# Two loops written out, and the halo copies shared between ScalarE and SyncE, in a four-layer convolution network

## The chip, the cores and the metric

The kernel runs on one core of one Trainium2 chip. Its engines are TensorE (PE in the profile; PEld is its weight load), VectorE (DVE), ScalarE (ACT), GpSimd (POOL) and SyncE (SP), which run side by side, each through its own list of instructions, and meet at semaphores. ScalarE and SyncE can also issue DMA transfers (ACTq, SPq). The metric is the device time of one execution in microseconds; lower is better.

## What is computed

The input is 64 images of 16 channels of 128 x 128 in float32. Four layers follow, each `x = x + f(group_norm(x))`, with eight groups of two channels:

```python
x = x + _L0_conv_ref(_gn(x), 5)      # Newton-Schulz inverse of each 128 x 128 matrix, 5 steps
x = x + _L1_conv_ref(_gn(x), ...)    # 3 x 3 convolution of x quantised with one scale for the whole batch
x = x + _L2_conv_ref(_gn(x), ...)    # convolution with five taps on a diagonal, zero padding
x = x + _L3_conv_ref(_gn(x), ...)    # circular 3 x 3 convolution (the reference takes it through FFTs)
```

Layer 1's scale is a maximum over all images, so layer 0 must be done for all of them before layer 1 starts for the first.

## The kernel before, in words

There are two blocks, one after the other.

The first does layer 0 image by image: `X` has four buffers (`SLOTS`), an image is 16 matrices of 128 x 128. TensorE multiplies (`products`, line 758; `last_products`, line 768), ScalarE takes the products out of PSUM (line 363), GpSimd forms the factor 2I - Y (line 288), the DVE finishes the image (line 528) and prepares the norms of the next (lines 425 to 482), whose broadcast on TensorE is line 742. SyncE loads image i+3 (line 243) and stores image i to a scratch tensor in device memory (line 249). Every engine runs the same function `step` for images 0, then a loop over images 1 to 60, then images 61 to 63. The loop (`images`, lines 80 to 85) is a hardware loop: `Fori` runs its body with a register, and the body has `turn` steps, here four, so it has 15 turns. Inside it, semaphore counts and addresses that depend on the image are computed in registers.

The second does layers 1 to 3 as a pipeline: at step s, image s is in layer 1, image s-1 in layer 2 and image s-2 in layer 3. The function `run` (lines 879 to 885) does steps 0 to 3, loops over steps 4 to 61 in turns of two, and does steps 62 to 65. An image lies in SBUF with 128 partitions = 8 rows x 16 channels, and 16 such blocks of rows in the free dimension. A convolution is a sum of matmuls in PSUM: the taps inside a block (line 1147), and then one product with the halo, the rows just above and below each block (line 1154). The halo lies in `xh`, six groups of 16 partitions, filled by six SBUF-to-SBUF copies: three groups from the block above, three from the block below. All six are issued by ScalarE in `halos` (line 939), for layer 3 after the circular wrap of the edges (`wrap`), for layer 1 when the DVE has quantised the next image (line 1003), for layer 2 when GpSimd has written the lower half of the fp16 split (line 920). ScalarE's other work in a step is a root for each norm (line 962), the upper half of the split (line 957), and a bias (line 969). SyncE only loads image s+2 from the scratch tensor (line 897) and stores image s-2 (line 908).

The order on each engine is the order written in its `step`. On TensorE it is: layer 1, layer 2, layer 3, each in four banks, with the small matmuls of the norm statistics (lines 1160 and 1165) put in between.

Of the kernel before, what the change touches and what calls it, by code (L numbers as in the profile page):

```python
# [20 lines left out]
C = 16  # L21
G = 8
CPG = C // G
RB = 8
NJ = H // RB
PW = H + 4
L = 2
# [7 lines left out]
SLOTS = 4  # L35
# [10 lines left out]
def conv_net(nc, x, ident, gmat, gsel, w1, w1h, w2, w2h, w3, w3h, scale_w, bias, x1d, out):  # L46
# [6 lines left out]
    B = x.shape[0]  # L53
# [23 lines left out]
        def wait(self):  # L77
            self.eng.wait_ge(self.sem, self.at)

    def images(eng, step, first, last, turn):  # L80

        assert (last - first) % turn == 0
        with eng.Fori(0, (last - first) // turn) as t:
            for a in range(first, first + turn):
                step(t * turn + a, t + a // turn, a % turn)

    keep = ExitStack()
    with keep:
# [36 lines left out]
        xn = [None] + [[persistent(f"xn{l}_{n}", [H, parts[l], FLAT], kinds[l]) for n in range(2)] for l in (1, 2, 3)]  # L125
# [15 lines left out]
        with mem:  # L141
# [80 lines left out]
            A_FIRST, A_LAST = 1, 3  # L222

            def image_steps(eng, step):

                for i in range(A_FIRST):
                    step(i, 0, i)
                images(eng, step, A_FIRST, B - A_LAST, SLOTS)
                for i in range(B - A_LAST, B):
                    step(i, i // SLOTS, i % SLOTS)  # L230

# [4 lines left out]
            with nc.Block() as block:  # L236

                @block.sync
                def _(sp):
                    def load(n, h, slot):  # L240
                        stand(sp, x1_stored[slot], 16 * h, const_loaded, 16 * 5)
                        stand(sp, reached, n - 3, const_loaded, 16 * 5)
                        sp.dma_start(X[slot][:, :, :], x[n, :, :, :]).then_inc(x_loaded[slot], 16)

                    def step(i, h, slot, last=False):
                        if not last:
                            load(i + 3, h + (slot + 3) // SLOTS, (slot + 3) % SLOTS)
                        stand(sp, out_ps, QUADS * (i + 1), const_loaded, 16 * 5)
                        sp.dma_start(x1d[i, :, :, 0:H].rearrange("j (r c) w -> (j r) c w", c=C),
                                     X[slot][:, :, :]).then_inc(x1_stored[slot], 16)  # L250

                    for t, s in ((idt, ident), (gm, gmat), (gs, gsel), (swt, scale_w), (bst, bias)):
                        sp.dma_start(t[:, :], s).then_inc(const_loaded, 16)
                    load(0, 0, 0)
                    load(1, 0, 1)
                    load(2, 0, 2)
                    for l, body, rows in ((1, w1, w1h), (2, w2, w2h), (3, w3, w3h)):
                        sp.dma_start(wf[l][:, :, :], body).then_inc(w_loaded, 16)
                        sp.dma_start(whf[l][:, :], rows).then_inc(w_loaded, 16)
                    for i in range(A_FIRST):  # L260
                        step(i, i // SLOTS, i % SLOTS)
                    images(sp, step, A_FIRST, B - A_LAST, SLOTS)
                    for i in range(B - A_LAST, B):
                        step(i, i // SLOTS, i % SLOTS, last=i + 3 >= B)
                    for n in range(SLOTS):
                        sp.wait_ge(x1_stored[n], 16 * (B // SLOTS))
# [568 lines left out]
        RUN = NJ * PW - (PW - H)  # L835
        HALO1 = [(-1, d, 0) for d in (-1, 0, 1)] + [(RB, d, RB - 1) for d in (-1, 0, 1)]
        HALO = (None, HALO1, HALO2, HALO1)
        with ExitStack() as mem:
# [7 lines left out]
            xh = [None] + [[sb(f"xh{l}_{n}", [6 * C, parts[l], NJ * PW], kinds[l]) for n in range(2)] for l in (1, 2, 3)]  # L846
# [16 lines left out]
            normed = [None] + [sem(f"normed{l}") for l in (1, 2, 3)]  # L863
            wrapped = sem("wrapped")
# [12 lines left out]
            FIRST = 4  # L877

            def run(eng, step):

                for s in range(FIRST):
                    step(s, s // 2, s % 2)
                images(eng, step, FIRST, B - 2, 2)
                for s in range(B - 2, B + 2):
                    step(s, s // 2, s % 2)

            def there(i):

                return not isinstance(i, int) or 0 <= i < B

            with nc.Block() as block:

                @block.sync
                def _(sp):
                    def load(n, h, odd):
                        stand(sp, evac[1], BPI * (n - 1), w_loaded, 16 * 6)
                        sp.dma_start(xs[1][odd][:, :, :],
                                     x1d[n, :, :, 0:H].rearrange("j p w -> p j w")).then_inc(x1_in[odd], 16)

                    load(0, 0, 0)  # L900
                    load(1, 0, 1)

                    def step(s, h, odd):
                        if there(s + 2):
                            load(s + 2, h + 1, odd)
                        if there(s - 2):
                            stand(sp, evac[3], BPI * (s - 1), w_loaded, 16 * 6)
                            sp.dma_start(out[s - 2, :, :, :], xs[3][odd][:, :, :]).then_inc(out_stored[odd], 16)

                    run(sp, step)  # L910
                    for n in range(2):
                        sp.wait_ge(out_stored[n], 16 * (B // 2))
# [19 lines left out]
                @block.scalar  # L932
                def _(act):
                    def halos(l, n, odd):

                        for k, (row, shift, _) in enumerate(HALO[l]):
                            r, at = (row + RB, 0) if row < 0 else (row - RB, 2 * PW)
                            at += L + shift
                            act.dma_start(xh[l][odd][C * k:C * k + C, :, 0:RUN],  # L939
                                          xn[l][odd][C * r:C * r + C, :, at:at + RUN]).then_inc(halo[l][odd], 16)  # L940

                    def wrap(i, odd):

                        v = xn[3][odd][:, :, :].rearrange("p s (j w) -> p s j w", w=PW)
                        link = Link(act, wrap_chain, 2 * i)
                        act.wait_ge(normed[3], i + 1)
                        link.done(nc.scalar.activation(v[:, :, 1:NJ + 1, L - 1], v[:, :, 1:NJ + 1, L + H - 1],
                                                       ACT.Copy))
                        link.done(nc.scalar.activation(v[:, :, 1:NJ + 1, L + H], v[:, :, 1:NJ + 1, L], ACT.Copy))
                        link.wait()  # L950
                        nc.scalar.activation(v[:, :, 0, :], v[:, :, NJ, :], ACT.Copy).then_inc(wrapped, 1)
                        nc.scalar.activation(v[:, :, NJ + 1, :], v[:, :, 1, :], ACT.Copy).then_inc(wrapped, 1)

                    def upper(l, n, odd):

                        act.wait_ge(scaled_f[l], n + 1)
                        nc.scalar.activation(padded(xn[l][odd], 0)[:, 1:NJ + 1, L:L + H], F[l][:, :, :],  # L957
                                             ACT.Copy).then_inc(high[l], 1)

                    def root(l, n):  # L960
                        act.wait_ge(gvar_sb[l], n + 1)
                        nc.scalar.activation(cols[l]["sd"][:, :], cols[l]["ve"][:, :],  # L962
                                             ACT.Sqrt).then_inc(groot[l], 1)

                    def first(n, h, odd):

                        act.wait_ge(normed[1], n + 1)
                        halos(1, n, odd)
                        nc.scalar.activation(xs[1][odd][:, :, :], xs[1][odd][:, :, :], ACT.Identity,
                                             bias=bst[:, 0:1]).then_inc(biased, 1)  # L970

                    def step(s, h, odd):
                        if there(s - 2):
                            wrap(s - 2, odd)
                            act.wait_ge(wrapped, 2 * s - 2)
                            halos(3, s - 2, odd)
                        if there(s):
                            root(2, s)
                            upper(2, s, odd)
                        if there(s + 1):  # L980
                            first(s + 1, h + odd, 1 - odd)
                        if there(s):
                            act.wait_ge(normed[2], s + 1)
                            halos(2, s, odd)
                        if there(s - 1):
                            root(3, s - 1)
                            upper(3, s - 1, 1 - odd)

                    first(0, 0, 0)
                    run(act, step)  # L990
# [263 lines left out]
```

## Time and profile before

| | us |
|---|---|
| three runs, median (lowest, highest) | 4625.2 (4619.82, 4630.58) |
| the profiled execution | 4624.59 |
| its span, first to last instruction | 4622.8 |
| mean granted TensorE clock | 0.986 of full |

The page of the profile begins with the busy time of each engine, then the span in 40 equal slices (busy share in tenths; PEclk is the granted clock of TensorE):

```profile
PE 4399.1 (95%) x24265; PEld 3045.4 (66%) x24265; DVE 3833.0 (83%) x8224; ACT 2251.8 (49%) x4551; POOL 2610.2 (56%) x2957
...
PE   7999999999999999999999599999999999999998
...
PEclk9999999999999999999999799999999999999999
DMA  1111111111111111211111365555556555555554
```

The first block fills some 22 slices, the second the rest. Of the queues of the page, q1 and q10 are data transfers, q8 and q14 instructions being fetched:

```profile
q1 hardware_dynamic: 284112, 269.46, 18.2%
q10 hardware_dynamic: 49152, 129.59, 16.8%
q8 instruction: 165, 2.70, 0.2%
q14 instruction: 162, 1.33, 0.1%
```

The chain of work that ended last, by engine:

```profile
PE 39%; DVE 3%; issue 1%; ACTq 0%; DMA 0%; ACT 0%; POOLq 0%; POOL 0%
```

### The profile page before, as it was taken

The page shows a single profiled execution, that of the slowest core. Times are in us where ns is not written, and L with a number is a line of the kernel's source. Part 1 is how long each engine was busy: PE and PEld are TensorE (multiplying, and loading weights), DVE is VectorE, ACT ScalarE, POOL GpSimd, SP SyncE. Part 2 cuts the span into 40 slices and gives each one's busy share as a digit, 9 for nine tenths or more (in the row PEclk, how much of TensorE's full clock was granted, in tenths as well). Part 3 has the DMA queues.
Part 4 walks back from the last instruction along what each step waited for, and adds up shares of the span by engine and source line. Part 5 has one row for each costly group of instructions (what it writes and reads, how often), then busy time and mean ns, then how long its engine had stood idle before and what let it go on. Part 6 is the DMA issues. An engine that isn't in the chain of part 4 may idle for free. (4 is left out here: it accounts for less than half of the span.)

```text
span 4622.8 us, 79863 instructions
## 1 busy us (share of the span) xinstructions
PE 4399.1 (95%) x24265; PEld 3045.4 (66%) x24265; DVE 3833.0 (83%) x8224; ACT 2251.8 (49%) x4551; POOL 2610.2 (56%) x2957
## 2 busy tenths in 40 slices
PE   7999999999999999999999599999999999999998
PEld 6888888888888888888888244444444444444443
DVE  7988898889888988988896687787787778778774
ACT  4766776777677766777776122222222222222221
POOL 7888888888888888888887122222222222222221
PEclk9999999999999999999999799999999999999999
DMA  1111111111111111211111365555556555555554
GB/s 59 61 48 56 56 56 56 56 56 56 56 56 56 56 56 47 63 49 56 56 56 37 84 137 130 130 134 137 125 132 139 127 130 136 132 128 134 137 127 85
DMA packets 333591, 403.08 MB, mean 87 GB/s; under 512 B 23088, under 2 KB 286032, under 8 KB 316880
## 3 DMA queue, kind: packets, MB, share of 16 engines
q1 hardware_dynamic: 284112, 269.46, 18.2%
q10 hardware_dynamic: 49152, 129.59, 16.8%
q8 instruction: 165, 2.70, 0.2%
q14 instruction: 162, 1.33, 0.1%
HBM read 135.22 MB, written 134.22 MB: 58 GB/s over the span
## 5 line engine op out<-in xcount | busy, mean ns | idle before, releaser
L288 POOL TENSOR_TENSOR M<-two,YX 128x256 f32<-128x256 f32 x2560 | 1827.0, 741 | 402.6 <-ACT YX L363 373.4
L758 PE MATMUL bank<-YX,M 128*128 128x256 f32 x8192 | 1948.5, 386 | 40.1 <-issue 40.1
L1147 PE MATMUL bank<-xn,wt 128*128 128x512 f16 (+1 forms) x6912 | 1660.2, 381 | 25.6 <-DVE xn L1003 17.9
L758 PEld LDWEIGHTS bank<-YX,M 128*128 128x128 f32 x8192 | 1504.1, 192 | 227.3 <-issue 44.5
L363 ACT ACTIVATE YX<-bank 128x512 f32<-128x512 f32 x2048 | 1227.5, 599 | 690.8 <-PE bank L758 684.8
L920 POOL TENSOR_TENSOR xn<-F,xn 128x2048 f16<-128x2048 f32 x128 | 487.8, 3811 | 1577.6 <-ACT xn L957 1577.6
L1147 PEld LDWEIGHTS bank<-xn,wt 128*128 128x128 f16 (+1 forms) x6912 | 672.9, 100 | 810.5 <-issue 18.8
L1021 DVE SCALAR_TENSOR_TENSOR x<-bank,wu,x 128x512 f32<-128x512 f32 x512 | 382.2, 746 | 294.7 <-PE bank L1154 283.8
L1154 PE MATMUL bank<-xh,wth 96*128 96x512 f16 (+1 forms) x1792 | 515.4, 380 | 15.3 <-DMA xh<-xn 15.3
L957 ACT ACTIVATE xn<-F 128x2048 f16<-128x2048 f32 x128 | 244.7, 1912 | 475.1 <-DVE F L1077 475.1
L410 DVE BATCH_NORM_STATS2 st<-X 128x6 f32<-128x256 f32 x1024 | 367.8, 410 | 9.6 <-DMA X<-in_x 9.6
L471 DVE TENSOR_SCALAR W<-X,m,r 128x256 f32<-128x256 f32 x512 | 363.3, 778 | 12.3 <-DVE r L463 12.1
L1032 DVE BATCH_NORM_STATS2 bs<-x 128x6 f32<-128x512 f32 x512 | 355.5, 694 | 17.6
L962 ACT ACTIVATE sd<-ve 128x1 f32<-128x1 f32 x128 | 26.0, 203 | 692.6 <-issue 363.0
L1154 PEld LDWEIGHTS bank<-xh,wth 96*128 96x128 f16 (+1 forms) x1792 | 174.4, 97 | 235.1 <-DMA xh<-xn 18.0
L354 ACT ACTIVATE YX<-bank,cs 128x128 f32<-128x128 f32 x1024 | 318.0, 389 | 10.7 <-DVE cout L497 10.0
L528 DVE SCALAR_TENSOR_TENSOR X<-bank,cout,X 128x128 f32<-128x128 f32 x1024 | 270.5, 342 | 40.6 <-PE bank L768 40.6
L282 POOL TENSOR_TENSOR W<-W 128x512 f16<-128x512 f32 x256 | 298.3, 1166 | 6.0 <-ACT W L332 6.0
L339 ACT ACTIVATE AD<-X,nm 128x256 f32<-128x256 f32 x512 | 256.7, 503 | 33.4 <-DVE nm L428 33.4
L768 PE MATMUL bank<-YX,M 128*128 128x128 f32 x2048 | 250.4, 280 | 0.0
L768 PEld LDWEIGHTS bank<-YX,M 128*128 128x128 f32 x2048 | 238.4, 192 | 3.3
L729 PE MATMUL bank<-W 128*128 128x128 f16 x3072 | 215.2, 220 | 2.3 <-ACT YX L354 2.3
(107 smaller groups left out, 3580.6 us busy)
## 6 DMA issues: line engine op xcount, KB each, us to landing
xh<-xn ACTq DMA_DIRECT2D x768, 131.8 KB, 4.3
X<-in_x SPq DMA_DIRECT2D x64, 1024.0 KB, 4.8
x_scratch<-X SPq DMA_DIRECT2D x64, 1024.0 KB, 5.7
x<-x_scratch SPq DMA_DIRECT2D x64, 1024.0 KB, 6.1
out<-x SPq DMA_DIRECT2D x64, 1024.0 KB, 3.8
xh<-xn ACTq DMA_DIRECT2D x384, 65.9 KB, 2.4
wf<-in_w SPq DMA_DIRECT2D x2, 192.0 KB, 8.5
wf<-in_w SPq DMA_DIRECT2D x1, 320.0 KB, 8.5
```

The lines of the kernel that those rows point to most:

```text
L288: nc.gpsimd.tensor_tensor(M[odd][:, at, :], two[:, :].unsqueeze(1).broadcast_to([H, 2, H]), YX[odd][:, at, 0:H], ALU.subtract).then_inc(ma ...
L354: ins = nc.scalar.activation(YX[odd][:, mat, 0:H], bank[:, m * H:(m + 1) * H], ACT.Copy, scale=cs[odd][:, mat:mat + 1])
L363: nc.scalar.activation(YX[odd][:, 2 * p:2 * p + 2, :], banks[u % A_RING][:, :].rearrange("p (m w) -> p m w", m=2), ACT.Copy).then_inc(yx_n ...
L410: ins = nc.vector.bn_stats((st0, st1)[k][:, g, :], group_of(X[slot], g))
L471: ins = nc.vector.tensor_scalar(group_of(W, g), group_of(X[slot], g), m0[:, g:g + 1], r0[:, g:g + 1], ALU.subtract, ALU.mult)
L758: ins = nc.tensor.matmul(banks[u % A_RING][:, 2 * H * m:2 * H * (m + 1)], M[odd][:, 2 * p + m, :], YX[odd][:, 2 * p + m, :], start=True, s ...
L768: ins = nc.tensor.matmul(banks[q][:, H * m:H * (m + 1)], M[odd][:, 4 * q + m, :], YX[odd][:, 4 * q + m, H:2 * H], start=True, stop=True)
L920: nc.gpsimd.tensor_tensor(padded(xn[l][odd], 1)[:, 1:NJ + 1, L:L + H], F[l][:, :, :], padded(xn[l][odd], 0)[:, 1:NJ + 1, L:L + H], ALU.sub ...
L1021: nc.vector.scalar_tensor_tensor(out=dst, in0=bank, scalar=wtop[l]["u"][:, 0:1], in1=xs[l][odd][:, a:b, :], op0=ALU.mult, op1=ALU.add).the ...
L1032: nc.vector.bn_stats(bst_[l][:, u, :], xs[l][odd][:, 4 * u:4 * u + 4, :]).then_inc(gchain[l], 1)
L1147: nc.tensor.matmul(bank, wt[l][:, a, k, :], v, start=(k == a == b == 0), stop=False)
L1154: ins = nc.tensor.matmul(bank, wth[l][:, a, :], v, start=False, stop=(a, b) == products[-1])
```

## The change

`images` is now a loop of the program that writes the kernel: each of the 60 images of the first block and the 58 steps of the second stands in the instruction lists by itself, with constant semaphore counts and addresses. No hardware loop is left in these two places. In the second block the copies of the block above stay with ScalarE, and the three copies of the block below are issued by SyncE, which waits for the same events. The sum of the copies on each halo semaphore is as before.

```diff
-    def images(eng, step, first, last, turn):
-
-        assert (last - first) % turn == 0
-        with eng.Fori(0, (last - first) // turn) as t:
-            for a in range(first, first + turn):
-                step(t * turn + a, t + a // turn, a % turn)
+    def images(step, first, last, turn):
+
+        for i in range(first, last):
+            step(i, i // turn, i % turn)
...
                 def _(sp):
+                    def halos(l, n, odd):
+
+                        if l == 3:
+                            sp.wait_ge(wrapped, 2 * n + 2)
+                        else:
+                            sp.wait_ge(normed[l], n + 1)
+                        for k, (row, shift, _) in enumerate(HALO[l][3:]):
+                            r, at = row - RB, 2 * PW + L + shift
+                            to = C * (k + 3)
+                            sp.dma_start(xh[l][odd][to:to + C, :, 0:RUN],
+                                         xn[l][odd][C * r:C * r + C, :, at:at + RUN]).then_inc(halo[l][odd], 16)
+
...
                     load(1, 0, 1)
+                    halos(1, 0, 0)
 
                     def step(s, h, odd):
+                        if there(s - 2):
+                            halos(3, s - 2, odd)
                         if there(s + 2):
                             load(s + 2, h + 1, odd)
+                        if there(s + 1):
+                            halos(1, s + 1, 1 - odd)
+                        if there(s):
+                            halos(2, s, odd)
                         if there(s - 2):
                             stand(sp, evac[3], BPI * (s - 1), w_loaded, 16 * 6)
                             sp.dma_start(out[s - 2, :, :, :], xs[3][odd][:, :, :]).then_inc(out_stored[odd], 16)
...
-                        for k, (row, shift, _) in enumerate(HALO[l]):
-                            r, at = (row + RB, 0) if row < 0 else (row - RB, 2 * PW)
-                            at += L + shift
+                        for k, (row, shift, _) in enumerate(HALO[l][:3]):
+                            r, at = row + RB, L + shift
                             act.dma_start(xh[l][odd][C * k:C * k + C, :, 0:RUN],
                                           xn[l][odd][C * r:C * r + C, :, at:at + RUN]).then_inc(halo[l][odd], 16)
```

## Rows read from the trace of the kernel before

**Rows 1.** Busy time by stretch: us, each engine's busy us (instructions), clock, DMA share, GB/s.
```profile
3000.00:3500.00 500.00, 488.04 (x2308) 224.01 (x2307) 396.87 (x784) 119.36 (x144) 121.95 (x32) 1.00 0.58 132
```

**Rows 2.** Timeline of SyncE (start, duration, operation): stores of images 0, 3, 4, 5, 60.
```profile
88.31 0.65 SPq L249 DMA_DIRECT2D x_scratch<-X  x1
...
203.01 0.57 SPq L249 DMA_DIRECT2D x_scratch<-X  x1
...
240.56 0.56 SPq L249 DMA_DIRECT2D x_scratch<-X  x1
...
282.79 0.56 SPq L249 DMA_DIRECT2D x_scratch<-X  x1
...
2428.03 0.57 SPq L249 DMA_DIRECT2D x_scratch<-X  x1
```

**Rows 3.** Waits of TensorE, 88 to 2426 us: total us, times, longest.
```profile
PE bank L758 <- issue: 40.1, 17, 3.1
PE bank L742 <- DVE ndiag L482: 26.2, 26, 1.0
```

**Rows 4.** Timeline of TensorE across a jump back: start, duration, in brackets idle before.
```profile
235.74 3.19 PE L768 MATMUL bank<-YX,M 128*128 128x128 f32 x26
...
241.70 3.63 PE L758 MATMUL bank<-YX,M 128*128 128x256 f32 x8 [2.77 <-issue]
```

**Rows 5.** Busy time in the stretch behind that jump; the clock is third from last.
```profile
240.00:244.00 4.00, 2.30 (x6) 1.86 (x7) 2.19 (x3) 0.34 (x1) 0.00 (x0) 0.74 0.63 177
```

**Rows 6.** Line 428: duration in ns, min/median/max.
```profile
L428 DVE TENSOR_SCALAR nm<-mean x64: 172/565/3416, 99.5 to 2547.2; 128x8 f32 x60, 128x8 f32<-128x8 f32 x4
```

**Rows 7.** DMA queues (packets, MB, share) in 1200:1700, then 3000:3500, then from 4500.
```profile
q8 instruction: 32, 0.52, 0.4%
...
q10 hardware_dynamic: 12300, 32.45, 38.5%
q1 hardware_dynamic: 35328, 33.56, 19.9%
...
q8 instruction: 3, 0.05, 0.2%
```

**Rows 8.** Waits of TensorE, 2750 to 4500 us; this is the only row.
```profile
PE bank L1165 <- DVE q L1054: 41.8, 56, 0.8
```

**Rows 9.** Timeline of one step of the second block, from several engines.
```profile
3011.31 0.38 SPq L897 DMA_DIRECT2D x<-x_scratch  x1
...
3012.83 5.51 ACTq L939 DMA_DIRECT2D xh<-xn  x6
...
3020.11 1.23 DVE L1003 TENSOR_SCALAR xn<-T 128x2048 bf16<-128x2048 f32 x1
...
3025.58 3.81 POOL L920 TENSOR_TENSOR xn<-F,xn 128x2048 f16<-128x2048 f32 x1 [14.08 <-ACT xn L957]
3025.76 0.81 PE L1154 MATMUL bank<-xh,wth 96*128 96x512 f16 x3
...
3028.23 1.19 DVE L1045 TENSOR_SCALAR dv<-bs,m 128x8 f32<-128x8 f32 x1
...
3037.64 0.36 SPq L908 DMA_DIRECT2D out<-x  x1
```

**Rows 10.** Halo copies: size and us to landing; their issue and TensorE's waits, ends.
```profile
xh<-xn ACTq DMA_DIRECT2D x768, 131.8 KB, 4.3
...
xh<-xn ACTq DMA_DIRECT2D x384, 65.9 KB, 2.4
...
2571.49 3.81 ACTq L939 DMA_DIRECT2D xh<-xn  x6
...
2577.15 0.61 PE L1154 MATMUL bank<-xh,wth 96*128 96x512 bf16 x1 [4.17 <-DMA xh<-xn]
...
2598.07 0.61 PE L1154 MATMUL bank<-xh,wth 96*128 96x512 bf16 x1 [6.30 <-DMA xh<-xn]
...
4607.18 1.46 PE L1154 MATMUL bank<-xh,wth 96*128 96x512 f16 x3 [4.80 <-DMA xh<-xn]
```

More of the change, by code:

```diff
@@ L227, in image_steps @@
                     step(i, 0, i)
-                images(eng, step, A_FIRST, B - A_LAST, SLOTS)
+                images(step, A_FIRST, B - A_LAST, SLOTS)
                 for i in range(B - A_LAST, B):
@@ L261, in _ @@
                         step(i, i // SLOTS, i % SLOTS)
-                    images(sp, step, A_FIRST, B - A_LAST, SLOTS)
+                    images(step, A_FIRST, B - A_LAST, SLOTS)
                     for i in range(B - A_LAST, B):
@@ L882, in run @@
                     step(s, s // 2, s % 2)
-                images(eng, step, FIRST, B - 2, 2)
+                images(step, FIRST, B - 2, 2)
                 for s in range(B - 2, B + 2):
```

## The prediction

> **What bounds the kernel now.** I read the busy time by stretches first, then the waits of TensorE, then the timelines around its longest gaps, and last the DMA queues by stretch. The kernel has two halves. The first (the matrix inversions, up to 2535 us) and the second (the three convolutions, from 2571 us) are both bound by TensorE: in the second it works 488.04 of 500 us at the full clock [rows 1]. So only what changes TensorE's idle time or its clock can move the end.
>
> In the first half the stores of image 0 and image 60 stand 2428.03 - 88.31 = 2339.72 us apart for 60 images [rows 2], exactly the images that the loop runs over, in 15 turns of four with 14 jumps back. Inside a turn the period is 37.55 us (203.01 to 240.56); over a jump it is 42.23 us (240.56 to 282.79) [rows 2]. TensorE's waits in that stretch are of two sorts only: 40.1 us in front of line 758, released by nothing that the profile knows ("issue"), and 26.2 us in 26 waits of 1.01 us for the DVE's diagonal, line 482 [rows 3]. The 17 waits of the first sort hold three very short ones; the other 14 are the jumps. At one of them the last products end at 238.93 and the first product of the next turn starts 2.77 us later [rows 4], after which the clock is low for a while: 0.74 of full on average over 240 to 244 us, that is the 1.2 GHz level for about half of the time [rows 5]. So a jump costs the idle time, and some half-speed work behind it.
>
> The other sort of wait is a two-state thing. Line 428, a DVE operation on 8 elements, takes 0.57 us in the median image, 0.17 at the least and 3.42 at the most [rows 6]. When it is long, the chain to line 482 ends late and TensorE waits 1.01 us. In the second half the same pattern is plain: GpSimd's line 920 runs from 3025.58 to 3029.39, and the DVE's line 1045, started at 3028.23, ends at 3029.42 though an operation on so few elements can be done in 0.17 us [rows 6, 9]. That delays the statistics matmul of layer 3 by 0.75 us in each of 56 steps (41.8 us) [rows 8]; 16 of them are the whole 12.0 us that TensorE is idle in 500 us [rows 1].
>
> **Part 1, the first loop written out.** It removes the jumps, and the registers with their additions, which run in the sequencers beside the engines; I cost these at nothing, because TensorE has no wait of that sort inside a turn [rows 3]. The work of an image does not change. Sixty images at the short period are 60 x 37.55 = 2253.0 us. The 26 waits for the diagonal add 26.2 us [rows 3]. What is left of 2339.7 is 60.5 us, or 4.3 us a jump: 40.1 us of it is the idle time of [rows 3], the other 20 us the slow clock behind the jumps. The image after a jump is almost always of the short kind, since the pause lets the DVE run ahead; without the jump it would be of either kind, about half of them long: 14 x 0.5 = 7 us given back. Gain 60.5 - 7 = 53.5 us, say 54.
> Its bounds come from the same two-state wait. If all sixty images fell into the long state, they would take 60 x 38.56 = 2313.6 us, a gain of 26 us; if all were short, 87 us. The states follow one another in the loop with no rule that I can see, so I take the mixture.
> The row shows the pause with a taken jump and none in the straight stretches. The Trainium skill, "Runtime: NRT & Kernel Launch", section "Instruction fetch mechanics", says the same in general: fetching ahead is sequential, and a taken branch to a place outside the engine's window must first fetch it. It also tells why the second loop, with its much shorter body, has no such pause: by it the jump there costs nothing, and my sum has nothing for it.
>
> **Part 2, the second loop written out.** Its jumps cost nothing now: TensorE's only waits from 2750 to 4500 us are the 56 of line 1165 [rows 8], one a step, and the two steps of a turn are alike. So there is nothing to gain. What it adds is instruction traffic: in 500 us of the first half the queue q8 fetches 32 blocks, while in 500 us of the second loop only the data queues q1 and q10 appear at all [rows 7]. The bounds of that cost are nothing (the straight code after the loop, from 4500 us, fetches three blocks on q8 [rows 7], and the waits there have the last image's dependencies as their cause) and one stall for each block, which is a rival below. I take nothing, for the straight stretch is the nearer row.
>
> **Part 3, half of the halo copies from SyncE.** A step issues 18 copies from ScalarE: six for each layer. Six large ones take 5.51 us to issue (0.92 each) and land 4.3 us after issue; six small ones take 3.81 us (0.64 each) and land after 2.4 us [rows 9, 10]. Nine a step move to SyncE. In the steady state this is hidden. Layer 3's copies are issued from 3012.83 to 3018.34, the last has landed at about 3022, and its matmul (line 1154) runs at 3025.76 [rows 9]: 3.7 us of slack, and layers 1 and 2 have more. ScalarE's root for layer 2 waits behind that issue until 3018.4, but the DVE quantises the next image first, up to 3021.34 (line 1003 [rows 9]), so the 3 us that ScalarE gets back start nothing earlier; GpSimd's line 920 depends on that same DVE chain, so the 0.75 us stall stays. On SyncE the order by time is: wait for the wrap (3012.8), three copies, the load (now 3011.31 [rows 9], then some 3 us later), wait for layer 1's input (the end of line 1003, 3021.3), three copies, wait for layer 2's (the end of line 920, 3029.4), three copies, the store (3037.6) [rows 9]. Each wait ends before the next item would have been due. Behind the first wait stands the load, which the DVE needs only in the next step, some 30 us on; nobody waits for it. Cost nothing, with 1 us a step as the bound above: the copies of one layer would have to land 3.7 + 1 us later than now.
> The copies are exposed at three places: the halo of image 0 in layer 1 (TensorE waits 4.17 us), that of image 1 (6.30 us) and layer 3's of the last image (4.80 us) [rows 10]. For the small copies the issue is the pace: three instead of six end 3 x 0.64 = 1.9 us sooner. Twice that is 3.8 us, of which I keep 3.4, because layer 2 of image 0 is then next to be late. The large ones take half as long again to issue, 0.92 against 0.64 us by the same instruction, so their queue is partly held back by the transfers: between nothing and 3 x 0.92 = 2.8 us, I take 1.5, about the middle. Together 4.9, say 5 us, with bounds of nothing and 3.8 + 2.8 = 6.6 us.
> The stretched issue of the large copies speaks against more. The Trainium skill, "DMA: Bandwidth & Descriptors", section "Issuing engines are not separate DMA queues", says that copies from several engines share the same 16 DMA engines, and that issuing from two saves the sequencer's time alone. By that rule the large copies give nothing and this part is 3.4 us, not 4.9.
>
> **The sum.** 54 + 5 = 59 us. The profiled execution took 4624.6 us (span 4622.8 and 1.8 around it), 0.6 us under the median of 4625.2. 4624.6 - 59 = 4565.6; I say 4565.5 us.
>
> **The rivals.**
> (a) The two-state wait locks. With equal images and no pause to reset them, the engines may settle into one state. All long: 4624.6 - 26 - 5 = 4594 us. All short: 4624.6 - 87 - 5 = 4533 us. For it: nothing then differs from image to image. Against it: 26 waits in 60 images [rows 3] are a mixture though three images in four follow another without a jump.
> (b) Fetching in the second half stalls TensorE; this one ends on the other side. The place is each new block of TensorE's instructions between 2750 and 4560 us, where the data queues take 38.5% and 19.9% of the DMA engines' time [rows 7]. At the first half's rate (32 in 500 us, an upper end, as crossings fetch extra) that is up to 116 blocks. If each costs what a jump costs without the clock, 2.8 us, it is +325 us, 4890 us; the decision lies at 59 / 116 = 0.5 us a block. Against it: in the first half blocks are fetched beside 1 MB loads and stores with no wait at all, and the fetches are sequential, so that they can be early.
> (c) The copies from SyncE come too late in each step, by traffic or by the order of its waits. At 1 us in each of 62 steps it eats the gain: 4626 us, no change. Against it the slack of 3.7 us.
> (d) The pause is not the jump's but the work's at every fourth image (the fourth buffer X coming round). Then only part 3 stays: 4620 us, no change. Against it: the pause sits in front of a product that waits for nothing new, the profile names no engine or transfer that it was waiting for [rows 3, 4], and every image reloads one buffer, so that no image is special.
>
> **How the numbers follow.** The forecast (mixed states) 0.64, (a) long 0.12, (a) short 0.10, (b) 0.05, (c) 0.05, (d) 0.04. Of (b), mild forms below the decision point only shrink the gain. The range takes in both ends of (a) nearly: 4537 to 4598, the upper end with some microseconds for a mild (b) or (c). A measurement of this kernel tells about 0.2% (9 us) from no change. Faster by more than that: 0.64 + 0.22 and half of a mild (b) or (c), 0.89. Within it: 0.05. Slower: 0.06.
>
> **What the profile afterwards would show.** If part 1 is right, "issue" in front of the product line is gone from TensorE's waits, no interval between stores is over 39 us, and the clock stays at 1.00 in the first half; the number of waits for the diagonal tells the state. If part 2 is right, q8 appears in the second half and the waits of TensorE there are still only the statistics matmul's 0.75 us. If part 3 is right, the three exposed waits shrink and nothing else does. I am wrong if halo matmuls wait in the middle of the second half, if "issue" waits come up at equal distances there, or if the diagonal's waits number 60.

## The result and the profile after

| | us |
|---|---|
| before, median of the six runs beside it | 4625.7 |
| after, median of six runs (lowest, highest) | 4553.3 (4551.7, 4558.6) |
| ratio after to before | 0.9853, 95% interval 0.9836 to 0.9869 |
| the profiled execution after, and its span | 4556.3, 4554.5 |

One of the six runs of the kernel before took 18807.8 us and is left out of the ratio; the other five lie between 4610.3 and 4630.6 us. The kernel is 72 us faster by the medians, and 68 us (61 to 76) by the ratio; 4565.5 was forecast, with 4537 to 4598 as the range. From profiled span to profiled span it is 4622.8 - 4554.5 = 68.3 us. A second set of runs gave a ratio of 0.9843 (0.9826 to 0.9859).

The page of after begins so; TensorE does the same matmuls in 21.1 us less busy time. In the images of the first loop none of them runs behind a pause at half speed any more: the granted clock is 1.00 from 88 to 2364 us:

```profile
span 4554.5 us, 69799 instructions
PE 4378.0 (96%) x24265; PEld 3031.8 (67%) x24265; DVE 3841.3 (84%) x8224; ACT 2249.5 (49%) x4551; POOL 2606.1 (57%) x2957
...
q1 hardware_dynamic: 308688, 334.25, 29.5%
q10 hardware_dynamic: 24576, 64.79, 5.5%
```

Some 10,000 instructions are gone (the register work), and half of q10's packets have moved to q1, SyncE's.

**The first half.** SyncE's stores of images 0, 3, 4 and 60 after, which answer to [rows 2], and all of TensorE's waits in the stretch, which answer to [rows 3]:

```profile
89.29 0.66 SPq L247 DMA_DIRECT2D x_scratch<-X  x1
...
201.91 0.53 SPq L247 DMA_DIRECT2D x_scratch<-X  x1
...
239.46 0.53 SPq L247 DMA_DIRECT2D x_scratch<-X  x1
...
2364.18 0.53 SPq L247 DMA_DIRECT2D x_scratch<-X  x1
```
```profile
PE bank L740 <- DVE ndiag L480: 23.0, 23, 1.0
```

The "issue" waits are gone, and no interval between two stores is over 38.6 us. Images 1 to 60 take 2364.18 - 89.29 = 2274.89 us instead of 2339.72, 64.8 us less, and the short period is still 37.55 us (201.91 to 239.46). 60 x 37.55 + 23.0 = 2276.0 us: the short images and the long waits account for the whole stretch within 1.1 us. The second half begins (first matmul of layer 1) at 2507.5 instead of 2571.5 us.

**The second half.** In the middle nothing has changed. The busy time of 500 us answers to [rows 1], the wait to [rows 8] and the step to [rows 9]:

```profile
2930.00:3430.00 500.00, 487.91 (x2307) 223.67 (x2304) 396.20 (x785) 119.30 (x144) 122.40 (x33) 1.00 0.58 133
```
```profile
PE bank L1181 <- DVE q L1070: 42.0, 56, 0.8
```
```profile
2944.39 2.30 SPq L902 DMA_DIRECT2D xh<-xn  x3
2944.39 3.32 ACTq L955 DMA_DIRECT2D xh<-xn  x3
...
2946.78 1.35 SPq L907 DMA_DIRECT2D x<-x_scratch  x1
...
2957.93 3.81 POOL L937 TENSOR_TENSOR xn<-F,xn 128x2048 f16<-128x2048 f32 x1 [14.86 <-ACT xn L973]
...
2960.57 1.19 DVE L1061 TENSOR_SCALAR dv<-bs,m 128x8 f32<-128x8 f32 x1
```

SyncE and ScalarE start their three copies in the same moment, and the load comes behind them. The small operation of the DVE still lasts until GpSimd has finished (2961.7), and the statistics matmul still waits 0.75 us. The three exposed places, which answer to [rows 10], and one new wait (layer 2 of image 0):

```profile
2511.71 0.61 PE L1170 MATMUL bank<-xh,wth 96*128 96x512 bf16 x1 [2.78 <-DMA xh<-xn]
...
2530.88 0.61 PE L1170 MATMUL bank<-xh,wth 96*128 96x512 bf16 x1 [4.41 <-DMA xh<-xn]
2540.60 0.82 PE L1170 MATMUL bank<-xh,wth 96*128 96x512 f16 x3 [0.57 <-DMA xh<-xn]
...
4537.71 1.46 PE L1170 MATMUL bank<-xh,wth 96*128 96x512 f16 x3 [3.43 <-DMA xh<-xn]
```

From its first matmul to the end the second half takes 4554.5 - 2507.5 = 2047.0 us instead of 4622.8 - 2571.5 = 2051.3: 4.3 us less.

### The profile page after: what moved, and what is told of

Same layout as the page of the kernel before. It is cut to its first block and busy times, and to the rows that moved or that the text cites. A ratio compares the mean times of both kernels' runs of the same rounds, so it can differ in the third digit from the quotient of the medians.

```text
span 4554.5 us, 69799 instructions
## 1 busy us (share of the span) xinstructions
PE 4378.0 (96%) x24265; PEld 3031.8 (67%) x24265; DVE 3841.3 (84%) x8224; ACT 2249.5 (49%) x4551; POOL 2606.1 (57%) x2957
## 5 line engine op out<-in xcount | busy, mean ns | idle before, releaser
L469 DVE TENSOR_SCALAR W<-X,m,r 128x256 f32<-128x256 f32 x512 | 373.3, 798 | 2.3
```

The costliest lines, as they stand in the source:

```text
L469: ins = nc.vector.tensor_scalar(group_of(W, g), group_of(X[slot], g), m0[:, g:g + 1], r0[:, g:g + 1], ALU.subtract, ALU.mult)
```

## The experiments

**The parts alone.** Four kernels, each with part of the change. `a_only` writes out the first loop only, `b_only` the second only:

```diff
+    def straight(eng, step, first, last, turn):
+
+        for i in range(first, last):
+            step(i, i // turn, i % turn)
...
-                images(eng, step, A_FIRST, B - A_LAST, SLOTS)
+                straight(eng, step, A_FIRST, B - A_LAST, SLOTS)
```

`halo_only` keeps both loops and shares the copies; `loops_nosplit` is the changed kernel with `halos` of ScalarE as it was and none on SyncE.

> The kernel before with only the first loop written out; the second loop and the six copies from ScalarE stay. If the pause at a jump is the cause of the gain: 60 images take 2253 us plus 1.0 us for each long wait of line 742, the 40 us of 'issue' waits are gone, and the time is some 65 us under before, about 4561 us. If the halo copies or the second loop carried part of the gain, the time is over 4570 us. If the pause is the work's and not the jump's, no change.

> The kernel before with only the second loop written out. Theory: nothing, 4625 us within 2 us, with the instruction queue q8 now active in the second half and the same 31.2 us a step. Rival (fetching costs in the second half): slower by more than 5 us, with 'issue' waits of TensorE at equal distances. Rival (register work in the sequencers costed something): faster by some us, with a step under 31.2 us.

> The kernel before with only the copies shared between ScalarE and SyncE; both loops stay. Theory: 3 to 5 us faster, all of it at the three exposed places (first two images, last image); a step in the middle stays 31.2 us. Rival: the shared copies or SyncE's waits cost something in each step, visible as a step over 31.2 us. Rival: nothing at all, because the transfers and not their issue set the pace.

> Both loops written out, all six copies from ScalarE. Theory: the changed kernel plus the 4 us of the copies, 4557 to 4560 us. If the parts do not add up (a layout effect of the longer code), it differs from the sum of the single parts by over 5 us.

| kernel | ratio to before (95%) | images 1 to 60 | waits for the diagonal | second half |
|---|---|---|---|---|
| a_only | 0.9877 (0.9862 to 0.9892) | 2272.9 | 21 | 2050.9 |
| b_only | 0.9997 (0.9988 to 1.0007) | 2342.5 | 27 | 2051.0 |
| halo_only | 0.9981 (0.9972 to 0.9990) | 2341.1 | 28 | 2051.7 |
| loops_nosplit | 0.9871 (0.9857 to 0.9886) | 2290.4 | 39 | 2051.5 |

(The last three columns are of the profiled execution, in us; the ratio is of all runs.) The first loop carries the gain: 1.2% of 4626 is 57 us (59.5 by the medians), where 65 were expected. The profiled execution of `a_only`, 4554.7 us, is its fastest; two of its four runs are over the 4570 us above which the expectation would have had another part carry some of the gain. `loops_nosplit`, expected at 4557 to 4560 us, took 4570.05: it does what the two single loops add up to, but the changed kernel is faster than it by more than the expected cost of the copies. The second loop carries nothing, although its instructions are now fetched too (18 blocks on q8 in 500 us in the middle):

```profile
q8 instruction: 18, 0.29, 0.2%
```

and its only wait there is that of the statistics matmul, 42.7 us in 57. That settles rival (b) for this kernel: 18 blocks in 500 us, none with a wait. Rival (d) is contradicted by `a_only`, where the pause went with the loop alone.

The sharing of the copies is worth 0.19% or 8.8 us in the median, more than the 3 to 5 expected, but its profiled execution shows no gain in the second half at all. What was gained at the first two images was lost at the next:

```profile
2596.60 3.02 SPq L904 DMA_DIRECT2D xh<-xn  x3
2596.60 4.31 ACTq L957 DMA_DIRECT2D xh<-xn  x3
2600.33 0.38 SPq L909 DMA_DIRECT2D x<-x_scratch  x1
...
2607.10 1.46 PE L1172 MATMUL bank<-xh,wth 96*128 96x512 f16 x3 [4.94 <-DMA xh<-xn]
```

One of ScalarE's issues took 2.31 us (the longest; 0.65 is the median), so its third copy left at 2599.65, beside the load of 1 MB that SyncE issued at 2600.33, and landed 7.4 us later. In the changed kernel the load is issued 2.5 us after the last copy, that copy lands in 5.6 us, and the wait is 0.57 us. That the load was what held the copy up is read from these two executions and was not tested; if so, the gain of the sharing at the start depends by microseconds on what it meets.

**The two-state wait.** The column of waits explains the differences in the first half. TensorE's waits there, for the changed kernel shown above, then a_only, then loops_nosplit:

```profile
PE bank L747 <- DVE ndiag L487: 21.0, 21, 1.0
```
```profile
PE bank L740 <- DVE ndiag L480: 39.0, 39, 1.0
```

60 x 37.55 + 21 = 2274 (measured 2272.9), + 39 = 2292 (2290.4), + 23 = 2276 (2274.9). So these three kernels have the same images, and in their profiled executions they differ by the number of long waits at 1.0 us each. The control below asked whether that number belongs to the code:

> The changed kernel itself once more, as the control of the three beside it: 4551 to 4571 us. If the number of long waits of line 740 (the diagonal) is a matter of chance from execution to execution, its time spreads over 10 us and the profiled one shows a number other than 23, at 1.0 us each. If the number belongs to the code, it is 23 again.

It ran at 4554.7 us (4553.7 to 4558.8), with images 1 to 60 in 2275.8 us and 24 of them long in the profiled execution: close to 23, not equal. All ten runs of the changed kernel lie in 7 us; the four of a_only spread from 4554.7 to 4573.4, and the four of loops_nosplit lie between 4563.8 and 4574.9. The number varies by execution, but its usual size seems to differ by kernel too, though the program of the first half is the same in all three. Why, none of the runs tells.

**What a jump costs.** Two more kernels vary only the length of a turn. `a_turn12` has 5 turns of 12 images, `b_turn8` has turns of 8 steps in the second loop, with the first six written out:

```diff
-                images(eng, step, A_FIRST, B - A_LAST, SLOTS)
+                images(eng, step, A_FIRST, B - A_LAST, 12, SLOTS)
```
```diff
-            FIRST = 4
+            FIRST = 6
...
-                images(eng, step, FIRST, B - 2, 2)
+                images(eng, step, FIRST, B - 2, 8, 2)
```

> The kernel before with the first loop in 5 turns of 12 images instead of 15 of 4; still a hardware loop with its registers. Theory (the cost sits at the jump, 4.3 us each): 4 jumps are left of 14, 10 x 4.3 = 43 us faster, within 10 us for the two-state wait; four 'issue' waits of some 2.8 us, 12 images apart. Rival (the pause belongs to every fourth image, when the buffers come round): still 14 pauses, no gain. Rival (the register work costs too): the images inside a turn are longer than in the written-out kernel.

> The kernel before with the second loop in turns of 8 steps instead of 2, so that its body has some 2400 TensorE instructions instead of 611 (steps 4 and 5 written out; 7 turns, 6 jumps). Theory (a jump costs where the body is fetched anew): the instruction queue q8 is active in the second half, and at the six jumps TensorE loses between 0 and 3 us each, less than in the first half, because its list of issued work before the jump is longer; 0 to 18 us slower. Rival (a jump costs by itself, whatever the length): no fetches and nothing at the jumps, as before.

`a_turn12`: ratio 0.9906 (0.9890 to 0.9923), 43.5 us faster, where 43 were expected; its images 1 to 60 took 2293.2 us. In its first half these are all the waits:

```profile
PE bank L743 <- DVE ndiag L483: 24.2, 24, 1.0
PE bank L759 <- issue: 12.3, 5, 3.1
```

Five "issue" waits in place of 17 (four pauses of 2.7 to 3.1 us and one of 0.7 behind the first). The pause goes with the jump, not with the buffers' round.

`b_turn8`: ratio 1.0021 (1.0011 to 1.0032), 9.7 us slower. Its ten runs fall into two groups, four from 4627.6 to 4632.4 us, which is where the kernel before lies, and six from 4641.1 to 4642.5; the profiled execution is one of the six, and what the other four did at their jumps is not known. In it the second half takes 2063.8 us against 2051.3. TensorE's waits from 2750 to 4500 us, and one of the six jumps:

```profile
PE bank L1166 <- DVE q L1055: 43.2, 56, 1.0
PE bank L1148 <- issue: 8.2, 6, 1.7
PE bank L1161 <- DVE s L1037: 1.4, 4, 0.5
```
```profile
3007.54 0.81 PE L1155 MATMUL bank<-xh,wth 96*128 96x512 f16 x3
3009.93 0.83 PE L1148 MATMUL bank<-xn,wt 128*128 128x512 bf16 x3 [1.58 <-issue]
```

The second loop's body had some 580 matmuls and weight loads (2308 and 2307 of them in 500 us [rows 1], 31.2 us a step, two steps a turn), and its jumps cost nothing. With a body four times as long it pays at every jump, and it has fetches all the way: 66 blocks on q8 between 2900 and 4400 us, where the short body had none [rows 7]. The body of the first loop, four images, has some 1880 (14106 and 14105 from 88 to 2364 us of the changed kernel). There q8 fetched 148 blocks between 88 and 2426 us before and 121 for the same work after: 27 more, about two for each of the 14 jumps.

The traces also hold the jump itself. It is one branch instruction in TensorE's own list (PEldq, the list with the weight loads). First the branches of the kernel before in its first loop, then in its second, then those of `b_turn8` in its second (duration in ns, min/median/max, start of the first and the last in us):

```profile
L83 PEldq COMPARE_BRANCH  x15: 79/3539/3829, 237.9 to 2425.4; - x15
```
```profile
L83 PEldq COMPARE_BRANCH  x29: 83/215/248, 2750.8 to 4498.9; - x29
```
```profile
L84 PEldq COMPARE_BRANCH  x7: 83/4976/5376, 3004.4 to 4516.1; - x7
```

The shortest of each row is the last one, which falls through. In the other engines' lists the same branch never takes over 0.07 us. During each of the long ones, 14 in the first loop and 6 in `b_turn8`'s second, exactly one block starts on q8: 0.9 to 1.5 us after the branch began in the first loop and 2.3 to 2.9 us in `b_turn8`. The branch ends 1.3 to 1.8 us after that block has landed. The block during the branch at 237.9 us [rows 4] (237.9 to 241.4 us), and the one during that at 3004.4 us of `b_turn8` (3004.4 to 3009.6 us; packets, MB, share):

```profile
q8 instruction: 1, 0.02, 2.1%
...
q8 instruction: 1, 0.02, 1.1%
```

No block comes on q8 between 2750 and 4500 us in the kernel before, where the branch takes 0.2 us. So a jump is dear when its target must be fetched anew, and TensorE's branch lasts until then. What TensorE loses is the part of the branch that is not covered by matmuls it already has. At 237.9 us it works until 238.93, which covers 1.0 of 3.5 us, and at 3004.4 us until 3008.35, which covers 3.9 of 5.3. That is the reason given in the expectation for the smaller loss in the second half.

**Two waits that the prediction found and the change left.** Both can be moved under other work by where TensorE's list has the small matmul. On top of the changed kernel:

```diff
-                            if prep and p == 7:
-                                norm_broadcast(i + 1)
                         for p in range(PAIRS):
                             products(i, odd, 2, p)
+                            if prep and p == 0:
+                                norm_broadcast(i + 1)
```
```diff
                                 conv(3, s, s - 2, h - 1, odd, u,
-                                     (lambda: mean(3, s - 1)) if u == 1 and there(s - 1) else None)
-                                if there(s - 1) and u == 1:
-                                    var(3, s - 1)
+                                     {1: lambda: mean(3, s - 1), 2: lambda: var(3, s - 1)}.get(u)
+                                     if there(s - 1) else None)
```

The first is `nb_later`, the second `var_later`, the two together `both_later`.

> The changed kernel, with TensorE's broadcast of the diagonal put one product later (behind the first product of the third step of the iteration), so that a late diagonal is hidden. Theory (each long wait costs 1.0 us and nothing else changes): the 60 images take 2253 us whatever the DVE does, 20 to 40 us less than the changed kernel, and the spread of the runs shrinks to some 3 us. Rival: the later broadcast delays the scale on the DVE and another wait takes its place; then the time is the same or worse.

> The changed kernel, with layer 3's second statistics matmul put between the taps of the third bank instead of behind the second. Theory: the 0.75 us stall in each of 62 steps is there only because GpSimd's subtraction holds up the DVE's small operation; 2 us later its result is there, a step takes 30.46 instead of 31.21 us, and the kernel is 46 us faster. Rival: the root and the normalisation of layer 3 come later, and the shorter step makes the halos late (slack was 3.7 us): less than 30 us gained, with waits of the halo matmul in the middle.

> Both of the two moves beside it in one kernel. Theory: they act in different halves and add up: 70 us under the changed kernel, about 4485 us. Rival: as in the single ones.

`var_later`: 4488.5 us, ratio 0.9699 (0.9683 to 0.9716), 66 us under the control `after_again`, where 46 were expected. (Its profiled execution, 4501.2 us, is the slowest of the four.) The middle of its second half:

```profile
3000.00:3500.00 500.00, 500.00 (x2387) 232.96 (x2385) 412.13 (x811) 123.41 (x147) 125.66 (x33) 1.00 0.60 137
...
3013.00 3.81 POOL L937 TENSOR_TENSOR xn<-F,xn 128x2048 f16<-128x2048 f32 x1 [14.45 <-ACT xn L973]
...
3015.65 1.18 DVE L1061 TENSOR_SCALAR dv<-bs,m 128x8 f32<-128x8 f32 x1
```

TensorE has no wait left there. The DVE's operation is still held up until GpSimd ends (3016.8), but nobody waits for it. A step takes 30.20 us instead of 31.22, 1.01 less where 0.75 was expected: the idle time was not the whole price of the stall. Over 62 steps that is 63 us, and the second half is 61.9 us shorter (1985.1 for 2047.0).

`nb_later`: 4549.4 us, ratio 0.9827 (0.9810 to 0.9843), 5 us under the control where 20 to 40 were expected, and the two intervals overlap. The diagonal's wait went, and half of it came back three products on, at the mean of the image after next:

```profile
PE bank L692 <- DVE st L408: 15.2, 27, 0.6
PE bank L740 <- DVE ndiag L480: 0.5, 3, 0.2
```

The rival holds, and for all of it: images 1 to 60 took 2273.9 us, where the changed kernel took 2274.9 and 2275.8. A long image still takes 1.03 us more than a short one (38.46 against 37.43), though its wait is now 0.56 us. In a long image the DVE is late for more than one customer, and what TensorE waits is not the whole of what the image loses. `both_later` took 4488.2 us (ratio 0.9695, 0.9678 to 0.9712): no different from `var_later`. Of the 70 us expected, the 66 of the second move are there; nothing of the first is.

**What holds up the DVE.** `nm_psum` is `var_later` with the operation of line 428 made straight from PSUM:

```diff
-                            nc.vector.tensor_scalar(nm1[:, :], mean, -1.0, None, ALU.mult).then_inc(neg_mean, 1)
+                            nc.vector.tensor_reduce(nm1[:, :], halves(k, 0), AX.X, ALU.add,
+                                                    negate=True).then_inc(neg_mean, 1)
```

> The kernel var_later, with the negated mean (the DVE operation on 8 elements that takes 0.2 to 3.4 us) made straight from PSUM by a reduction, so that it reads nothing from SBUF. Theory (that operation is held up by GpSimd through a path to SBUF that both use): it takes some 0.2 us in every image, and the long waits for the diagonal go or become rare: 60 images in 2255 to 2265 us, some 25 us under var_later. Rival (the next operation, which reads two SBUF tiles, is held up in its place): that one takes 3 us in the long images, and the number of long waits is as before.

The rival holds. The operation now takes 0.17 us in every image, and the next one, which reads two SBUF tiles, takes its place beside GpSimd's run of eight operations (3.33 us here, 0.16 at the least):

```profile
L426 DVE TENSOR_REDUCE nm<-bank x64: 173/174/176, 99.3 to 2567.5; 128x8 f32<-128x16 f32 x64
...
98.54 5.68 POOL L286 TENSOR_TENSOR M<-two,YX 128x256 f32<-128x256 f32 x8
...
99.40 3.33 DVE L428 TENSOR_TENSOR dev<-st,mean 128x16 f32<-128x16 f32 x1
```

The waits even grew (59.8 us in 37), and images 1 to 60 took 2357.5 us where `var_later` took 2284.5; ratio 0.9919 (0.9889 to 0.9950), some 90 to 100 us over `var_later`, where 25 under it were expected. So the stall is not of that one operation: it goes to whichever DVE operation on SBUF comes next while GpSimd works without a gap. Why, no run here shows directly. The Trainium skill has a reason in "SBUF — State Buffer", section "Terms": the DVE and GpSimd share one pair of SBUF ports, held by one of them for a whole instruction. The traces agree as far as they go: 0.17 us in all 64 images for the operation that reads PSUM, where from SBUF it took up to 3.42 [rows 6], and small operations that end within 0.03 us of GpSimd's [rows 9].

**The sharing in a shorter step.** `var_nosplit` is `var_later` with all six copies from ScalarE.

> The kernel var_later with all six copies from ScalarE again. Theory: the second half 3 to 5 us longer (var_later: 1985.1 us from its first matmul to the end), all of it at the first two images and the last one; a step stays 30.20 us. Rival: in the shorter step the slower issue of six copies makes halos or the root late, and a step is over 30.20 us.

Ratio 0.9755 (0.9738 to 0.9771) against 0.9699: 26 us slower, where 3 to 5 were expected. Its second half takes 2000.1 us against 1985.1, and a step 30.33 us against 30.20: the rival holds. Of the 15.0 us some 7 are in the steps of the middle, and 6.1 lie between the first matmul and the store of image 0 (92.7 against 86.6 us). TensorE waits 2.9 us in all for the DVE between 2690 and 4380 us, and the DVE for ScalarE's root. That line, first of `var_nosplit`, then of `var_later`:

```profile
DVE ra L1065 <- ACT sd L960: 94.3, 56, 2.7
```
```profile
DVE ra L1083 <- ACT sd L978: 18.1, 55, 0.4
```

The root stands behind the issue of the copies in ScalarE's list. With six copies it is 1.7 us late in a step on average, with three 0.3; in the kernel before, with six copies and the longer step, 0.6. So ScalarE's issue time, which was free in the step of 31.2 us, is no longer free in one of 30.2. In the profiled executions another 6.4 us are in the first half (39 long waits against 33, and images 1 to 60 in 2290.9 against 2284.5 us). The two profiled executions are 22.1 us apart.

## Why the prediction was right

**Part 1**, forecast 54 us, measured 64.8 between profiled executions. The mechanism is shown: the pauses went with the first loop alone (`a_only`), in proportion to the jumps (`a_turn12`), and each is a branch of 3.4 to 3.8 us with a fetched block inside it. The 60.5 us for 14 jumps was right, and so was its split: TensorE's busy time fell by 21.1 us, where the prediction gave 20 us to the slow clock. Mis-sized was the term that was given back: 7 us for jump images that would turn long, which means 33 long images of 60. There were 23 (24 in the control, 21 and 39 in the kernels beside it), 3 us gained rather than 7 lost. The premise was sound: in the kernel before, 24 of the 46 intervals between stores without a jump are long ones, which leaves 2 of the 26 long waits for the 14 with a jump. What no row told is that the share would not stay at half, and none of the runs tells why it did not. So it is luck that this term was off by 10 us and not more; with the 39 of `loops_nosplit` it would have been off by 6 us the other way. The bounds of 26 and 87 us, which came from all-long and all-short, were drawn for just this and held in the profiled execution of every kernel whose first loop is written out, `nm_psum` apart.

**Part 2**, forecast nothing, measured nothing: 0.9997 (0.9988 to 1.0007). The nearer row, the straight code at the end, was the right one to take. The estimate of up to 116 blocks was too high; 18 in 500 us are some 65 between 2750 and 4560 us.

**Part 3**, forecast 5 us, measured 4.3 between the profiles. The single places were 4.17 - 2.78 = 1.4 and 6.30 - 4.41 = 1.9 us for the small copies (1.9 each by the issue time), less the 0.57 us of the new wait in layer 2 of image 0, which the step had named as next to be late, and 4.80 - 3.43 = 1.4 us for the large ones (1.5). The Trainium skill's rule ("DMA: Bandwidth & Descriptors", section "Issuing engines are not separate DMA queues") is that issuing from two engines saves issue time alone, and the prediction read it as giving the large ones nothing. In the trace ScalarE's issue shrank with them (from 5.5 us for six to 3.3 for three), so that there was issue time to save there too: the rule agrees, that reading of it does not. In the middle the slack of 3.7 us covered everything, as argued. By the runs rather than the profiles the sharing may be worth 9 us (`halo_only`), and the changed kernel is 8 to 13 us faster than `loops_nosplit` by the two ratios. Of the profiled executions' difference the second half shows 4.5 us (2047.0 against 2051.5) and the images of the first half 15.5, by their long waits. Over all kernels these follow no rule that the sharing would give: 23, 24, 33 and 28 with the copies shared, 39, 39, 26, 27 and 21 without. Whether sharing copies that are not even issued in the first half can change them, or whether it is the place of the code in memory, or chance over four runs, stays open.

**The sum** was 59 us, the measured gain 72.4 in the median: 10.8 us more in images 1 to 60 (10 of them from the long waits), 0.8 less in the rest of the first half and 0.6 less in part 3, which makes the 68.3 us between the spans; the other 4 us are there because the profiled execution of after is 3.0 us above its median and that of before 1.1 us below its own.

The rivals: (a) did not lock; (b) is refuted by `b_only` and (d) by `a_turn12`, whose pauses went from 14 to 4 while the buffers came round as before; (c) is refuted for this kernel, and for the shorter step of `var_later` the sharing even helps.

## What to carry to other kernels

Look at a hardware loop's jump on the engine that sets the pace, and at the duration of its branch: in this kernel, where the instruction queue was active inside the loop, each jump fetched anew and showed as an "issue" wait, and longer turns or written-out code won it back; where the queue was silent, writing out gave nothing. A wait of less than a microsecond that comes once a step is worth more than the transfers that look busy: moving one small matmul behind work that was there anyway gave 66 us, nearly as much as the whole change. Before shortening a step, ask which engine's issue time was free only because the step was long.

## What the runs showed of the hardware

- TensorE's branch back to the head of a loop took 0.2 us with a body of some 580 matmuls and weight loads, 3.4 to 3.8 us with 1880 and 4.8 to 5.4 us with four times 580, each long one with a block of instructions fetched inside it.
- A pause of TensorE can cost more than its length. Behind a jump of the first loop the clock fell in 9 of 14 cases (0.50 or 0.72 of full over the six us behind the branch) and stayed at 1.00 in 5. In `nm_psum` all but two of 37 pauses were of 1.6 us: 8 of its images took 39.1 us and 29 about 40.8, against 37.44 for a short one. The clock stayed at 1.00 behind the pause at 104.3 us and fell behind the one at 220.0, so the pause alone does not decide it. Behind waits of 1.01 us in the kernel before it stayed at full in the stretches read (1.00 from 137 to 143 us). The stretch of 4 us around the pause at 220.0, with the clock third from last (0.70 of full, between the levels of 2.4 and 1.2 GHz):

```profile
219.00:223.00 4.00, 3.05 (x10) 2.62 (x11) 3.83 (x16) 1.29 (x4) 1.01 (x3) 0.70 0.00 0
...
219.95 0.40 PE L741 MATMUL bank<-ndiag,ones 32*128 32x32 f32 x2 [1.59 <-DVE ndiag L481]
```

  In the second half, pauses of 1.2 to 1.7 us at the jumps of `b_turn8` left it at full at all six (1.00 from 3006 to 3014 us, for one).
- Moving a small matmul out of a stall of 0.75 us took 1.01 us off the step.
- An issue of one SBUF-to-SBUF copy took between 0.52 and 2.31 us in one kernel (median 0.65).
